# Cross attention on one core: the shift row c of groups 1 to 3, summed from weighed x folded to 64 partitions

## The reference

```python
q = jnp.einsum('bte,ef->btf', emb, Wq) + bq
k = jnp.einsum('bml,le->bme', latent, Wk) + bk
v = jnp.einsum('bml,le->bme', latent, Wv) + bv
scale = 1.0 / jnp.sqrt(jnp.asarray(E, dtype=q.dtype))
w = jnp.einsum('bte,bme->btm', q, k) * scale
w = jax.nn.softmax(w, axis=1)
pred = jnp.einsum('btm,bme->bte', w, v)
x = pred + emb
mu = jnp.mean(x, axis=-1, keepdims=True)
var = jnp.var(x, axis=-1, keepdims=True)
return (x - mu) * jax.lax.rsqrt(var + EPS) * gamma + beta
```

## Time and profile before

| | us |
|---|---|
| median of 3 runs | 142.14 |
| lowest, highest | 142.10, 142.41 |
| the profiled execution | 142.47 |
| its span, from first to last instruction | 140.7 |
| PE busy | 134.4 |
| DVE busy | 115.1 |
| ACT busy | 79.7 |
| POOL busy | 60.8 |

### The profile page before, as it was taken

How to read it: one execution, slowest core, us unless ns; L and a number is a source line. 1 busy time by engine, 2 the same in 40 slices (tenths; PEclk the granted TensorE clock), 3 DMA queues, 4 the chain that set the end, 5 groups by cost and what they waited for, 6 DMA issues and landing times.

```text
span 140.7 us, 2977 instructions
## 1 busy us (share of the span) xinstructions
PE 134.4 (96%) x1046; PEld 130.0 (92%) x1046; DVE 115.1 (82%) x224; ACT 79.7 (57%) x283; POOL 60.8 (43%) x61
## 2 busy tenths in 40 slices
PE   7999999999999999999999999999999999999940
PEld 7899999999998999999999999999999999998940
DVE  0689995996996779999999976878799976797983
ACT  4267098667276925567473829474746546386420
POOL 1000000037304581733839370629475643629791
PEclk9999999999999999999999999999999999999996
DMA  4999999985187595986978789697987987536314
GB/s 139 328 404 420 424 278 389 302 285 199 20 261 269 175 374 166 366 328 198 349 289 301 285 305 370 234 330 224 301 278 280 342 260 256 209 108 221 121 73 150
DMA packets 10814, 37.33 MB, mean 265 GB/s; under 512 B 1200, under 2 KB 1456, under 8 KB 10800
## 3 DMA queue, kind: packets, MB, share of 16 engines
q1 hardware_dynamic: 9424, 34.79, 71.6%
q10 hardware_dynamic: 1376, 2.36, 4.4%
HBM read 33.87 MB, written 3.28 MB: 264 GB/s over the span
## 4 chain that ended last, share of the span: by engine, by line
PE 89%; POOL 5%; issue 2%; ACT 1%; POOLq 0%; DVE 0%; DVEq 0%
PE ps_S L424 29%; PE ps_U L438 26%; PE ps_Y L459 10%; PE ps_U L397 6%; PE ps_Y L397 6%; POOL xT_in L979 3%; PE ps_Y L340 2%; POOL xT_in L967 2%; PE ps_S L345 1%; PE ps_w L447 1%; PE ps_U L504 1%; PE ps_c L412 1%; PE ps_S L351 1%; PE ps_U L351 1%; ACT xT_in L601 1%
## 5 line engine op out<-in xcount | busy, mean ns | idle before, releaser
L583 ACT ACTIVATE expo<-scores,negmax 121x100 f32<-121x100 f32 x96 | 35.0, 365 | 31.0 <-DVE negmax L754 30.9
L424 PE MATMUL ps_S<-G,ctxT_in 128*121 128x100 f32 (+1 forms) x384 | 43.4, 269 | 0.0
L424 PEld LDWEIGHTS ps_S<-G,ctxT_in 128*121 128x121 f32 (+1 forms) x384 | 42.1, 185 | 0.0
L438 PEld LDWEIGHTS ps_U<-prob,ctx_in 121*128 121x128 f32 x336 | 39.4, 192 | 0.9
L438 PE MATMUL ps_U<-prob,ctx_in 121*128 121x100 f32 x336 | 39.6, 274 | 0.0
L956 POOL TENSOR_TENSOR prob<-expo,rinv 121x600 f32<-121x600 f32 x16 | 19.2, 1202 | 30.4 <-DVE rinv L761 30.2
L967 POOL TENSOR_TENSOR xT_in<-x_in,xT_in 128x512 f32<-128x512 f32 (+1 forms) x13 | 17.1, 1315 | 19.8 <-issue 8.9
L750 DVE TENSOR_TENSOR scores<-ps_S,c_rows 121x600 f32<-121x600 f32 x16 | 12.5, 782 | 10.1 <-PE ps_S L424 7.4
L765 DVE TENSOR_REDUCE probsum<-prob 121x100 f32<-121x600 f32 x16 | 19.8, 1239 | 1.0 <-POOL prob L956 0.7
L583 ACT ACTIVATION_READ_ACCUMULATOR expo<-scores,negmax 121x1 f32 x96 | 17.9, 187 | 0.0
L972 POOL TENSOR_TENSOR rstd<-vareps,neg_half 128x1 f32<-128x1 f32 (+1 forms) x13 | 7.1, 549 | 23.3 <-DVE vareps L792 23.1
(11 more groups left out here) (120 smaller groups left out, 184.4 us busy)
## 6 DMA issues: line engine op xcount, KB each, us to landing
ctx_in<-ctx SPq DMA_DIRECT2D x16, 768.0 KB, 5.2
ctxT_in<-ctxT SPq DMA_DIRECT2D x16, 722.0 KB, 5.1
xT_in<-xT SPq DMA_DIRECT2D x8, 400.0 KB, 8.6
x_in<-x SPq DMA_DIRECT2D x12, 256.0 KB, 4.5
out<-xT_in ACTq DMA_DIRECT2D x8, 256.0 KB, 4.1
wqk<-Wqk SPq DMA_DIRECT2D x4, 388.0 KB, 4.6
out<-xT_in SPq DMA_DIRECT2D x3, 256.0 KB, 2.0
wv_in<-Wv SPq DMA_DIRECT2D x1, 512.0 KB, 16.3
```

Of the source, the lines that this page charges most:

```text
L424: last = nc.tensor.matmul(ps_scores(c)[0:rows(c), :], ctxT_in[:, q, l * M + c * MP:l * M + c * MP + rows(c)], G[:, l, bass.ds(b * T, T)], ...
L438: last = nc.tensor.matmul(ps_U[:, q, l * T:(l + 1) * T], ctx_in[0:rows(c), q, c, l * P:(l + 1) * P], prob[0:rows(c), q, c * T:(c + 1) * T] ...
L583: last = nc.scalar.activation(expo[0:MP, q, c * T:(c + 1) * T], scores[0:MP, q, c * T:(c + 1) * T], ACT.Exp, bias=negmax[0:MP, q, c:c + 1] ...
```

## The change

Group 0 keeps its two halves and two matmuls. For groups 1 to 3 weighed x is first folded: ACT copies its upper 64 partitions to xu_upper on the lower ones (`lift`), and POOL adds them to the lower 64 (`fold_shift`), which gives xu_fold, 64 x 400. ACT rounds that into the lower 64 partitions of xu_parts (`upper_shift`), and POOL writes what the rounding left out into its upper 64 (`lower_parts`). One matmul of ones over all 128 partitions then sums both halves at once. The DVE subtraction is left only for group 0. On ACT the lift takes the place of the former copy, and the rounding copy stands further down; sum_shift(3) and take_shift(3) move one turn later.

```diff
+        xu_fold = sb("xu_fold", [P // 2, GT])
+        xu_upper = sb("xu_upper", [P // 2, GT])
+        xu_parts = sb("xu_parts", [P, 2, GT], F32R)
...
             def sum_shift(g):
 
                 pe.wait_ge(xuhi_set, g + 1)
-                pe.wait_ge(xulo_set, g + 1)
                 if g >= 1:
+                    pe.wait_ge(parts_lo_set, g)
                     pe.wait_ge(c_set, g)
+                    nc.tensor.matmul(ps_c[:, 0:GT], ones_r[:, :], xu_parts[:, g % 2, :], start=True, stop=True).then_inc(c_summed, 1)
                 else:
+                    pe.wait_ge(xulo_set, 1)
                     pe.wait_ge(onesr_set, 1)
-                nc.tensor.matmul(ps_c[:, 0:GT], ones_r[:, :], xu_hi[:, g % 2, :], start=True, stop=False)
-                nc.tensor.matmul(ps_c[:, 0:GT], ones_r[:, :], xu_lo[:, g % 2, :], start=False, stop=True).then_inc(c_summed, 1)
+                    nc.tensor.matmul(ps_c[:, 0:GT], ones_r[:, :], xu_hi[:, :], start=True, stop=False)
+                    nc.tensor.matmul(ps_c[:, 0:GT], ones_r[:, :], xu_lo[:, :], start=False, stop=True).then_inc(c_summed, 1)
...
             each_turn(turn, 5, 11)
+            turn(11, 1)
             sum_shift(3)
-            each_turn(turn, 11)
+            each_turn(turn, 12)
...
-            def upper_shift(g):
+            def lift(g):
                 act.wait_ge(xu_step, EC * (g + 1))
                 if g >= 2:
-                    act.wait_ge(c_summed, g - 1)
-                nc.scalar.activation(xu_hi[:, g % 2, :], xu[:, (EC - 1) % 2, :], ACT.Copy).then_inc(xuhi_set, 1)
+                    act.wait_ge(xu_folded, g - 1)
+                nc.scalar.activation(xu_upper[:, :], xu[P // 2:P, (EC - 1) % 2, :], ACT.Copy).then_inc(xu_lifted, 1)
+
+            def upper_shift(g):
+                if g == 0:
+                    act.wait_ge(xu_step, EC)
+                    nc.scalar.activation(xu_hi[:, :], xu[:, (EC - 1) % 2, :], ACT.Copy).then_inc(xuhi_set, 1)
+                else:
+                    act.wait_ge(xu_folded, g)
+                    if g >= 3:
+                        act.wait_ge(c_summed, g - 1)
+                    nc.scalar.activation(xu_parts[0:P // 2, g % 2, :], xu_fold[:, :], ACT.Copy).then_inc(xuhi_set, 1)
...
             take_group(2)
-            upper_shift(1)
+            lift(1)
             act.wait_ge(wv_loaded, 16)
             nc.scalar.activation(Wv_hi[:, :, :], wv_in[:, :, :], ACT.Copy).then_inc(Wvhi_set, 1)
+            upper_shift(1)
             exponentials(1, 1)
             take_group(3)
             act.wait_ge(rows_in, 48)
-            upper_shift(2)
+            lift(2)
             upper_U(0, 0)
             exponentials(2, 0)
             take_shift(1)
+            upper_shift(2)
             value_bias(0)
...
             each_turn(turn, 5, 9)
+            lift(3)
+            turn(9, 1)
             upper_shift(3)
-            turn(9, 1)
             turn(10, 0)
+            turn(11, 1)
             take_shift(3)
-            each_turn(turn, 11)
+            each_turn(turn, 12)
...
-            lower_shift(0)
+            lower_shift()
...
-            lower_shift(1)
             weigh_by_u(2)
             maxima(2, 0)
             lower_U(0, 0)
-            lower_shift(2)
             chunk_sum(1, 1)
...
             turn(9, 1)
-            lower_shift(3)
...
+            def fold_shift(g):
+                pool.wait_ge(xu_step, EC * (g + 1))
+                if g >= 2:
+                    pool.wait_ge(parts_lo_set, g - 1)
+                pool.wait_ge(xu_lifted, g)
+                nc.gpsimd.tensor_tensor(xu_fold[:, :], xu[0:P // 2, (EC - 1) % 2, :], xu_upper[:, :], ALU.add).then_inc(xu_folded, 1)
+                pool.wait_ge(xu_folded, g)
+
+            def lower_parts(g, probs):
+                pool.wait_ge(prob_set, probs)
+                pool.wait_ge(xuhi_set, g + 1)
+                nc.gpsimd.tensor_tensor(xu_parts[P // 2:P, g % 2, :], xu_fold[:, :],
+                                        xu_parts[0:P // 2, g % 2, :].bitcast(F32), ALU.subtract).then_inc(parts_lo_set, 1)
+                pool.wait_ge(parts_lo_set, g)
+
             pool.wait_ge(mask_set, 2)
             pool.wait_ge(consts_set, 2)
+            fold_shift(1)
             turn(1, 1)
+            lower_parts(1, 1)
             pool.wait_ge(Wvhi_set, 1)
...
-            each_turn(turn, 2)
+            turn(2, 0)
+            fold_shift(2)
+            lower_parts(2, 2)
+            each_turn(turn, 3, 9)
+            fold_shift(3)
+            turn(9, 1)
+            turn(10, 0)
+            lower_parts(3, 10)
+            each_turn(turn, 11)
```

More of the change, by code:

```diff
@@ L87, in xattn @@
         xu = sb("xu", [P, 2, GT])
-        xu_hi = sb("xu_hi", [P, 2, GT], F32R)
-        xu_lo = sb("xu_lo", [P, 2, GT], F32R)
+        xu_hi = sb("xu_hi", [P, GT], F32R)
+        xu_lo = sb("xu_lo", [P, GT], F32R)
+        xu_fold = sb("xu_fold", [P // 2, GT])
+        xu_upper = sb("xu_upper", [P // 2, GT])
+        xu_parts = sb("xu_parts", [P, 2, GT], F32R)
         G = sb("G", [P, LC, B * T])
@@ L149, in xattn @@
         xu_step = sem("xu_step")
+        xu_lifted = sem("xu_lifted")
+        xu_folded = sem("xu_folded")
+        parts_lo_set = sem("parts_lo_set")
         xuhi_set = sem("xuhi_set")
@@ L725, in weigh_by_u @@
             def weigh_by_u(g, terms=tuple(range(EC))):
-                if g >= 1 and 0 in terms:
-                    dve.wait_ge(xulo_set, g)
+                if g == 1 and 0 in terms:
+                    dve.wait_ge(xulo_set, 1)
+                if g >= 2 and 0 in terms:
+                    dve.wait_ge(xu_folded, g - 1)
                 for e in terms:
@@ L735, in weigh_by_u, with lower_shift @@
                                                        xu[:, (e - 1) % 2, :], ALU.mult, ALU.add).then_inc(xu_step, 1)
[L737 to L742, removed]
+            def lower_shift():
+                dve.wait_ge(xuhi_set, 1)
+                nc.vector.tensor_tensor(xu_lo[:, :], xu[:, (EC - 1) % 2, :], xu_hi[:, :].bitcast(F32),
+                                        ALU.subtract).then_inc(xulo_set, 1)
             def maxima(b, q):
```

## The result

The changed kernel is slower: 145.19 us (143.90 to 145.92, 6 runs) against 142.27 (141.65 to 142.78, 6 runs), a ratio of 1.020 with a 95% interval of 1.0147 to 1.0253. The forecast was 141.84, with a range up to 142.4. The profiled execution took 144.89 us, its span 143.2.

A forecast was written before the change was run, and what follows sets the result against it. PE was taken to bound the kernel, other engines' waits counting only if they reach it. Matmul savings of 0.55 us and a 0.25 stall gave -0.30, applied to the median of 142.14: 141.84 us, range 141.5 to 142.4.

The forecast's parts named there:

- two terms that were too small: PE stalls before scores(3) near 40 us, 0 to 0.15, and before values(2) near 62 us, 0.25 within 0 to 0.5.
- late end: Latest time given for operations delayed from 30 us on: maxima(2) 1.2 later, residual(0) at 45.5, add_residual(0) 46.8, rinv(3) 50.5.
- the -0.30: Forecast net change: 0.55 us of PE matmul time saved, less a 0.25 stall before values(2).
- rival C: Near 62 us rinv(5) falls behind residual(2), lower_U(4) is late, PE stalls 0.4 to 0.6 more: about +0.3, 142.45; chance 0.18.
- Place two: 80 to 88 us: fold(3) delays reciprocal root, scaling and prob(8) by about 0.8; no stall expected, 0.1 at most.

The follow-up runs named there:

- run 3: Kernel before, with the matmul of the lower half of weighed x left out for groups 1 to 3, all else kept: 144.25 us, ratio 1.0129.
- run 7: Kernel before, without the lower-half matmul for groups 1 to 3 and with POOL's residual waiting for rinv of its turn: 141.8 us, ratio 0.9963.
- run 11: Changed kernel, residual behind rinv each turn, Wv_lo ahead of group 1's fold, lower_parts and rounding copies of groups 1 and 2 later: 141.93 us, ratio 0.9970.
- run 4: Kernel before, with one unused 0.17 us VectorE memset between lower_U(3) and the normaliser of batch 5: 144.9 us, ratio 1.0173.
- Run 9: Changed kernel, last two weigh_by_u terms of group 3 moved before turn 9, its lift, fold and rounding copy one turn later: 143.42 us, ratio 1.0103.
- run 6: Changed kernel, with POOL waiting for rinv only in turn 6, ahead of residual(2): 142.77 us, ratio 1.0023.
- run 5: Changed kernel, with POOL's residual in each turn waiting for rinv of the same turn: 142.19 us, ratio 0.9996.
- run 2: Changed kernel, with group 3 put back to two matmuls, the VectorE subtraction and its old place: 145.56 us, ratio 1.0233.

## Why the prediction was wrong

**What held, and two terms that were too small.** PE's work fell as summed, though its busy time does not show it (134.4 in both): from scores(0) to scores(3) it took 20.15 before and 19.97 in runs 3, 7 and 11, 0.18 less for one matmul. POOL's new operations took 1.03 to 1.06 us for an estimate of 1.03. rinv(1) stood behind Wv_lo for 1.85 us (1.6 expected), the first term after it was short, and prob(1) then stopped the later terms: 2.79 us for 1.98. With scores(0) 0.61 earlier in that execution, maxima(2) at 39.20 answers to 39.8, 1.3 later than before where 0.2 to 1.2 stood. residual(0) answers to 45.8 (late end 45.5), add_residual(0) at 46.60 to 47.2 (late end 46.8), and rinv(3), under residual(1) as foreseen, ended at 50.9 (late end 50.5). So the chain was right and each link of it came 0.1 to 0.4 behind its late end. PE was idle for 0.29 before values(2), where 0.25 was summed; from start to start the stretch lost 0.60, so the term was less than half the cost, and above its end of 0.5. scores(3) cost 0.38 where 0 to 0.15 stood. These two alone would have turned the -0.30 into about +0.4, 142.6 us and already above the range.

The rules of the Trainium skill that the prediction weighed held here: "SBUF — State Buffer", Terms, has the loser of the shared port pair block completely, and rinv(1) ended 0.02 us behind Wv_lo (36.06 after 36.04); and "GPSIMD Engine Reference" (its table of the engine's properties) counts VectorE instructions with two SBUF inputs among those concerned. The trace of before had no such row for scalar_tensor_tensor; after the change one took 1.72 us under residual(3).

**The step that failed** is in the sum: it has no stall before values(3) and values(4), which then cost 1.42 and 1.01. The ground for putting them at nothing stands in rival C, which failed in its ground, its size and so its chance of 0.18. It said that rinv(5) and residual(2) "follow the same DVE work, so usually the order stays". They do not: residual(2) follows maxima(5) through ACT, rinv(5) follows the end of prob(4) on POOL, and maxima(5) had been waiting for PE. The prediction had used that PE would come 0.37 us earlier there, and DVE later, but looked only at margins that guard PE; that a wait of DVE for PE keeps two other engines in order was not looked for. Runs 3 and 4 show that either shift, PE two matmuls ahead (which moved the order by 0.18) or rinv(5) 0.07 later, is enough. Against a margin of 0.02 us with two different sources on its sides, and shifts of tenths that the prediction itself expected, a lost order deserved at least even odds, not 0.18.

**The size.** C was priced at +0.6 for lower_U(4) alone. The next residual was left out: with DVE 0.8 late, the third term no longer goes ahead of residual(3) but stands behind it, and the same again a turn later. Of the 1.42 the stretched term is 1.10 (1.72 for 0.62); the 0.3 that is left is near the 0.4 to 0.6 of C. Run 9 fits, without the terms there was no wait here, and so does run 6: with rinv(5) at 0.17 the terms stayed at 0.62. Priced so, C would have read +2.1 (-0.30 + 1.42 + 1.01) and not +0.3, and with the two early terms as measured about +2.9.

**Place two** came as described, and also above its end of 0.1: the values of turn 10 came 0.22 later. fold(3) held up the reciprocal root behind it, and over the scaling and prob(8) the lower_U(7) that values need:

```profile
83.62 1.05 POOL L1016 TENSOR_TENSOR xu_fold<-xu,xu_upper 64x400 f32<-64x400 f32 x1 [3.28 <-DVE vareps L815]
84.75 0.55 POOL L992 TENSOR_TENSOR rstd<-vareps,neg_half 128x1 f32<-128x1 f32 x1
```

It took both the fold and DVE's lateness from the turns before: run 5, with the fold and without the stretched terms, and run 2, with the stretched terms and without the fold, needed 12.03 and 12.01 for that stretch, as before.

**Still open.** The changed kernel's runs spread over 2 us (143.90 to 145.92) where those of before spread over 1.1; a race that falls either way in some executions would do that, but one execution's trace cannot show it.

## What to carry to other kernels

Where two engines block each other over a port, list the pairs whose order is fixed by timing alone, with the gap between them, and follow each side back to what releases it; a gap of some hundredths with different releasers is lost to any small shift on one side. It is no coin as long as the program stays the same: none of the 76 executions of the kernel before (141.56 to 142.96) shows the 2 us that the lost order costs. When the wrong order costs more than a wait, write the order down with a semaphore: one wait gave back 3 us here (145.19 to 142.19). And a kernel in which the bounding engine never waits can still lose from a saving on that engine, if its slowness was what kept the others in step.

## What the runs showed of the hardware

rinv, a VectorE operation of 0.17 us with both inputs in SBUF, lasts until the GpSimd operation ahead of it has ended: 1.85 us behind one of 2.36, 1.16 behind one of 1.29. A scalar_tensor_tensor of 0.62 us that is recorded 0.02 us ahead of the residual takes 1.72 us, while rinv(5), recorded 0.02 ahead of residual(2) in the kernel before, kept its 0.17: at such distances the recorded start does not tell who goes first. With a lead of 0.25 it was the residual that was stretched, from 1.28 to 1.50. Folding to half of the partitions buys GpSimd nothing (64 x 400 in 1.05 us lies on the line through 512 and 1024 columns of the earlier trace rows), nor ScalarE: the two copies took 0.54 and 0.53 us, the full one 0.54.
